# Graph attention and a top-2 expert network on one core: a new order of the attention steps, statistics of two tokens at once, a centred gate, and mixed tiles spread among the others

## The chip, the core and the metric

The kernel runs on one core of one Trainium2 chip. A core has five engines with instruction streams of their own: TensorE (PE, matmuls and transposes), VectorE (DVE), ScalarE (ACT), GpSimd (POOL) and SyncE (SP, which here issues DMAs). They meet only through semaphores. The metric is the device time of one execution in microseconds (us).

## The reference

There are 16384 tokens (128 graphs of 128 nodes) of 128 features, and 16 experts.

```python
def edge_score(a):
    s = jnp.einsum('bid,bjd->bij', hidden * a, hidden)
    return jax.nn.leaky_relu(s, LEAKY_SLOPE)
...
alpha = jnp.where(adj == 1, e0, NEG_INF)
alpha = jnp.where(adj == 2, e1, alpha)
...
alpha = jax.nn.softmax(alpha, axis=-1)
return jnp.matmul(alpha, hidden)
...
logits = jnp.einsum('bsd,de->bse', x, gate_w) + gate_b
probs = jax.nn.softmax(logits, axis=-1)
top_probs, top_idx = jax.lax.top_k(probs, 2)
...
h1 = jnp.einsum('bsd,edh->bseh', x, w1)
h2 = jnp.einsum('bsd,edh->bseh', x, w2)
hidden = jax.nn.silu(h1) * h2
expert_out = jnp.einsum('bseh,eho->bseo', hidden, w3)
...
x = x + _L0_gnn_ref(_layernorm(x, axis=-1), adj, L0_gnn_a0, ...)
x = x + _L0_ffn_ref(_layernorm(x, axis=-1), L0_ffn_gate_w, ...)
```

Each token needs only its two best experts.

## The kernel before

**Attention part.** The graphs are taken in 32 groups of four (`G`, `T`). `steps` writes the program of each engine step by step: in step `s` an engine does its work for several groups, each a fixed number of steps behind (`on(lag)`). The order inside a step is the order of the code, and each engine runs it strictly in turn. For a group, VectorE takes the statistics of each token (`bn_stats`, `bn_aggr`, L782 and L794), GpSimd makes scale and shift of them (`norm`, L533 to L546), ScalarE normalises (`h`, L624), TensorE transposes `h` into `psT` (L1004), and ScalarE copies that out as `hT` (L643) and four times scaled by `a0` to `a3` as `hTa` (L656). There is one buffer of each, so the scores of a group (L993, with the mask added by L997, into `psS`) must be done before those of the next are written. VectorE takes the largest of the four (L771, 2048 elements), the leaky slope (L788) and the row's maximum (L799), ScalarE the exponentials (L616). TensorE turns the probabilities (L1012) and multiplies (L1028), and VectorE adds the input (`x1`, L828). For the second layer norm there are statistics again (L844, L858), a normalised copy `x2` (L633), its transpose (L1020), the copy `x2T` (L653), the gate's matmul (L1058), `logit` (L850) and the two best experts (L865, L869). In every second step the places of two groups' tokens in their experts' lists are counted (L877 to L883, matmuls L1043 to L1049, L805 to L820). GpSimd then writes rows of 134 elements into `first_list` by indirect DMA (L559).

**Expert part.** Two passes (`r`), one for each of the two choices, have 72 tiles of 256 rows each. A *whole* tile belongs to one expert, a *mixed* one has two blocks of 128 rows with an expert each, a *lone* one holds the last incomplete blocks of two neighbouring experts. Each pass takes 48 whole, then 8 lone, then 16 mixed tiles, in turns of `S` = 8, with eight buffers (`xin`, `we`). SyncE reads a tile's word from a table with a register load (`value_load`, L398 and L401), loads its rows (L426 whole, L419 by blocks) and copies the expert's weights within SBUF into `we` (L415, 384 KB; a mixed tile does it twice). Buffer `u` is loaded again when its rows have been written out (`s_z[u]`). For tile `u` TensorE does the up-projections (L1101), then the transposes of tile `u + 1` (L1113), then the down-projection of tile `u - 1` (L1124). VectorE writes `hid` (L958), adds the result to the rows (L964) and, in the first pass, normalises the rows of tile `u + 2` (L971). GpSimd sends them to `second_list` (L571), in the second pass to the output (L583). The tiles of the first 4 turns are drawn from a list of the first 26 groups, so they can start before the others are sorted. Between the passes SyncE waits for the tiles with real rows, whose number for each buffer it reads from `real_i` (L466). ScalarE writes the padding rows during the tiles (L675, L680).

## Time and profile before

| what | us |
|---|---|
| median of 3 runs (822.02 to 825.97) | 824.17 |
| profiled execution | 820.67 |
| its span, first to last instruction | 818.7 |

| engine | busy us | share of the span |
|---|---|---|
| TensorE matmuls | 710.3 | 87% |
| TensorE weight loads | 572.1 | 70% |
| VectorE | 543.1 | 66% |
| ScalarE | 437.5 | 53% |
| GpSimd | 514.9 | 63% |

The shares are means over two parts with different limits, so each must be read by itself. A row of a timeline gives start, duration, engine, line, operation, what it writes and reads, and in brackets the idle time ahead of it with the engine or DMA that ended it. Merged rows (x4) span several instructions. The DMA engines moved 154.07 MB.

### The profile page before, as it was taken

How to read it: one execution, taken by the hardware profiler on the slowest of the kernel's cores; microseconds unless marked ns; L12 is line 12 of the kernel's file. 1: busy time of each engine (PE TensorE's matmuls, PEld its weight loads, DVE VectorE, ACT ScalarE, POOL GpSimd, SP SyncE). 2: the span in 40 equal slices, each digit the busy share in tenths (PEclk: the TensorE clock that was granted, in tenths of full speed). 3: DMA queues.
4: the chain of work that ended last, by engine and by line, in shares of the span. 5: the costliest groups of instructions: out<-in, count | busy, mean ns of one | idle time of the engine just before them, and what ended most of it. 6: DMA issues, size and time to landing. Idle time of an engine off the chain costs nothing.

```text
span 818.7 us, 17860 instructions
## 1 busy us (share of the span) xinstructions
PE 710.3 (87%) x4420; PEld 572.1 (70%) x4420; DVE 543.1 (66%) x2118; ACT 437.5 (53%) x1075; POOL 514.9 (63%) x664
## 2 busy tenths in 40 slices
PE   3788888888888887697999998977899999999872
PEld 1355555555555555586899998967799999999772
DVE  3779999999999999765666665543444444444231
ACT  4689999999999997232333332322233333333220
POOL 3124777777777777677767675654466666766443
PEclk9889999999999999589999999999999999999997
DMA  7233433332222210267999985888888888858880
GB/s 187 58 91 99 123 118 119 119 114 91 80 83 83 83 40 28 81 209 227 318 306 311 328 279 130 285 287 296 279 265 267 294 276 270 268 155 298 279 300 3
DMA packets 127449, 154.07 MB, mean 188 GB/s; under 512 B 16362, under 2 KB 98545, under 8 KB 127378
## 3 DMA queue, kind: packets, MB, share of 16 engines
q1 hardware_dynamic: 107008, 115.63, 44.5%
q0 software_dynamic: 15616, 34.38, 12.1%
q10 hardware_dynamic: 4754, 3.25, 1.3%
q8 instruction: 27, 0.44, 0.2%
q14 instruction: 44, 0.36, 0.2%
HBM read 52.28 MB, written 41.19 MB: 114 GB/s over the span
## 4 chain that ended last, share of the span: by engine, by line
POOL 28%; issue 27%; PE 20%; SPq 15%; DMA 4%; ACT 3%; DVE 1%; POOLq 1%; DVEq 0%; ACTq 0%
POOL first_list L559 14%; PE psS L1101 9%; SPq L419 5%; PE bank L1124 5%; POOL second_list L571 5%; SPq L415 5%; PE psS L993 4%; POOL norm L542 3%; SPq L401 3%; POOL out_dram L583 2%; ACT late L656 2%; DMA second_list<-xin 2%; PE bank L1113 1%; POOL stage L527 1%; POOL negmean L536 1%
## 5 line engine op out<-in xcount | busy, mean ns | idle before, releaser
L1101 PE MATMUL psS<-xT,late 128*128 128x256 f32 (+1 forms) x1280 | 249.8, 343 | 4.4 <-DMA late<-wts 2.3
L1101 PEld LDWEIGHTS psS<-xT,late 128*128 128x128 f32 x1280 | 202.7, 195 | 21.5 <-issue 4.5
L666 ACT ACTIVATE silu<-psS 128x512 f32<-128x512 f32 x144 | 86.0, 597 | 206.4 <-PE psS L1101 206.4
L583 POOL DMA_INDIRECT out_dram<-xin x144 | 141.6, 983 | 80.4 <-issue 53.5
L571 POOL DMA_INDIRECT second_list<-xin x144 | 141.9, 985 | 79.1 <-issue 52.0
L958 DVE TENSOR_TENSOR hid<-silu,psS 128x512 f32<-128x512 f32 x144 | 98.9, 687 | 134.5 <-PE psS L1101 127.9
L559 POOL DMA_INDIRECT first_list<-stage,slot x128 | 127.3, 994 | 50.3 <-issue 35.8
L993 PE MATMUL psS<-late,hT 128*128 128x512 f32 x256 | 126.6, 640 | 21.9 <-ACT late L656 20.8
L1124 PE MATMUL bank<-late,hid 128*128 128x128 f32 x1024 | 135.8, 276 | 0.1
L964 DVE SCALAR_TENSOR_TENSOR xin<-bank,xin 128x128 f32<-128x128 f32 x288 | 87.8, 346 | 70.3 <-PE bank L1124 64.9
L1124 PEld LDWEIGHTS bank<-late,hid 128*128 128x128 f32 x1024 | 124.6, 192 | 0.4 <-issue 0.4
L670 ACT ACTIVATE xT<-bank 128x256 f32<-128x256 f32 x144 | 55.4, 385 | 108.9 <-PE bank L1113 106.0
L993 PEld LDWEIGHTS psS<-late,hT 128*128 128x128 f32 x256 | 49.0, 202 | 76.8 <-issue 54.7
L771 DVE TENSOR_REDUCE late<-psS 128x512 f32<-128x2048 f32 x32 | 72.9, 2278 | 15.4 <-PE psS L997 14.0
L1113 PE MATMUL bank<-ident,xin 128*128 128x128 f32 x288 | 56.3, 277 | 28.5 <-DVE xin L971 18.2
L656 ACT ACTIVATE late<-bank,acol 128x512 f32<-128x512 f32 x128 | 76.9, 686 | 0.0
L1113 PEld LDWEIGHTS bank<-ident,xin 128*128 128x128 f32 x288 | 38.2, 143 | 42.5 <-issue 28.7
L971 DVE TENSOR_SCALAR xin<-xin 128x128 f32<-128x128 f32 x144 | 43.7, 375 | 24.9 <-DMA xin<-first_list 24.8
L624 ACT ACTIVATE h<-X,norm 128x128 f32<-128x128 f32 x128 | 52.7, 483 | 13.2 <-POOL norm L546 13.2
L542 POOL TENSOR_TENSOR norm<-veps,minus_half 128x8 f32<-128x8 f32 (+1 forms) x36 | 57.3, 1593 | 0.0
L533 POOL TENSOR_SCALAR veps<-mv 128x8 f32<-128x8 f32 (+1 forms) x36 | 9.5, 264 | 74.1 <-DVE mv L794 73.7
L633 ACT ACTIVATE x<-stage,norm 128x128 f32<-128x128 f32 x128 | 52.4, 480 | 4.1 <-POOL norm L546 4.1
(152 smaller groups left out, 913.4 us busy)
## 6 DMA issues: line engine op xcount, KB each, us to landing
late<-wts SPq DMA_DIRECT2D x160, 384.0 KB, 3.8
xin<-second_list SPq DMA_DIRECT2D x48, 262.0 KB
X<-in_x_dram SPq DMA_DIRECT2D x32, 256.0 KB, 2.9
late<-in_adj_dram SPq DMA_DIRECT2D x32, 256.0 KB, 3.4
xin<-first_list SPq DMA_DIRECT2D x48, 134.0 KB
xin<-second_list SPq DMA_DIRECT2D x48, 131.0 KB
wts<-in_L_ffn_w_dram SPq DMA_DIRECT2D x48, 128.0 KB
xin<-first_list SPq DMA_DIRECT2D x48, 67.0 KB
```

The source lines that it names most:

```text
L542: nc.gpsimd.tensor_tensor(norm[:, b, ln, :, 0], veps[:, b, ln, :], minus_half[:, ln, :], ALU.pow).then_inc(s_rs, 1)
L559: pool.indirect_dma_start(first_list[:, :], bass.IndirectOffsetOnAxis(ap=slot[:, g % SB, t:t + 1], axis=0), stage_v(g % SB)[:, t, :], None ...
L571: pool.indirect_dma_start(second_list[:, :], bass.IndirectOffsetOnAxis(ap=xin[:, u, k, SLOT1:SLOT1 + 1].bitcast(i32), axis=0), xin[:, u, k ...
L583: pool.indirect_dma_start(out_rows[:, :], bass.IndirectOffsetOnAxis(ap=xin[:, u, k, DEST:DEST + 1].bitcast(i32), axis=0), xin[:, u, k, 0:D ...
L656: last = nc.scalar.activation(hTa[:, k, :], psT[:, :], ACT.Copy, scale=acol[:, k:k + 1])
L666: nc.scalar.activation(silu[:, w, :], psG[w], ACT.Silu).then_inc(s_silu[u % TURNS], 1)
L958: v.tensor_tensor(hid[:, w, :], silu[:, w, :], psU[w], ALU.mult).then_inc(s_hid[u % TURNS], 1)
L964: last = v.scalar_tensor_tensor(at, psY[1 - w][:, t * D:(t + 1) * D], xin[:, k, t, GATE[r]:GATE[r] + 1], at, ALU.mult, ALU.add)
L993: mm(psS[:, t, :], hT[:, t * D:(t + 1) * D], hTa[:, :, t * D:(t + 1) * D], start=True, stop=False)
L1101: last = mm(out[:, c * W2 + rows.start:c * W2 + rows.stop], at[:, half * H + c * P:half * H + (c + 1) * P], xT[:, w, rows], start=True, st ...
L1113: last = nc.tensor.transpose(psX[1 - w][:, t * P:(t + 1) * P], xin[:, k, t, ROW:ROW2], ident[:, :])
L1124: last = mm(psY[1 - w][:, t * D:(t + 1) * D], hid[:, 1 - w, at:at + P], at_down[t][:, c * D:(c + 1) * D], start=(c == 0), stop=(c == HC - 1))
```

## The change

Attention part. `h` is normalised a step earlier: `steps` begins at -1, and statistics and `h` are those of group `s + 1`. TensorE transposes group `s` ahead of the scores of group `s - 1`. `hT` and `hTa` have two buffers, and ScalarE writes them ahead of the exponentials. Statistics are taken of two tokens with one instruction: their elements are read in turn, so that the even and the odd halves that `bn_stats` keeps are the two tokens' own, and `bn_aggr` goes. The gate is centred: the weights less their column means (`gwc`, made once) are applied to the transposed `x1` itself, and the scale is applied to the result (`scaled`), so `x2` goes. 

On ScalarE, one step of the attention part of before, `late<-late,negmax` being the exponentials, `late<-bank,acol` the scaled copies `hTa`, `x` the second normalised rows:

```order
L604 ACTIVATE late<-late 128x512
L616 ACTIVATE late,rowsum<-late,negmax 128x128 x4
L624 ACTIVATE h<-X,norm 128x128 x4
L633 ACTIVATE x<-stage,norm 128x128 x4
L643 ACTIVATE hT<-bank 128x512
L648 ACTIVATE probT<-bank 128x512
L653 ACTIVATE x2T<-bank 128x512
L656 ACTIVATE late<-bank,acol 128x512 x4
```

and the same step in the changed kernel:

```order
L613 ACTIVATE late<-late 128x512
L624 ACTIVATE hT<-bank 128x512
L626 ACTIVATE late<-bank,acol 128x512 x4
L634 ACTIVATE late,rowsum<-late,negmax 128x128 x4
L643 ACTIVATE h<-X,norm 128x128 x4
L651 ACTIVATE probT<-bank 128x512
L656 ACTIVATE x1T<-bank 128x512
```

The turned and scaled copies moved from the end of the step to its head, and the second normalisation is gone. On VectorE, from the reduction of the scores to the best experts in a step of before that does no counting:

```order
L771 TENSOR_REDUCE late<-psS 128x512
L777 RECIPROCAL rinv<-rowsum 128x4
L782 BN_STATS stats<-X 128x6 x4
L788 SCALAR_TENSOR_TENSOR late<-late 128x512
L794 BN_AGGR mv<-stats 128x2 x4
L799 TENSOR_REDUCE negmax<-late 128x4
L828 SCALAR_TENSOR_TENSOR stage<-bank,rinv,X 128x128 x4
L836 TENSOR_SCALAR late<-late 128x512 x4
L844 BN_STATS stats<-stage 128x6 x4
L850 TENSOR_TENSOR logit<-bank,gbias 128x64
L858 BN_AGGR mv<-stats 128x2 x4
L865 MAX best<-logit 128x8 x4
```

and in the changed kernel:

```order
L775 TENSOR_REDUCE late<-psS 128x512
L781 RECIPROCAL rinv<-rowsum 128x4
L747 BN_STATS stats<-X 128x6 x2
L793 SCALAR_TENSOR_TENSOR late<-late 128x512
L800 TENSOR_TENSOR scaled<-bank,norm 128x64
L806 TENSOR_REDUCE negmax<-late 128x4
L812 TENSOR_TENSOR logit<-scaled,gbias 128x64
L841 SCALAR_TENSOR_TENSOR stage<-bank,rinv,X 128x128 x4
L849 TENSOR_SCALAR late<-late 128x512 x4
L747 BN_STATS stats<-stage 128x6 x2
L865 MAX best<-logit 128x8 x4
```

Both aggregations went, four statistics became two, and the gate's sums take two operations, moved ahead of `x1`.

Expert part. `S` is 12, so there are twelve buffers. Only the up-projection's weights are copied (`UP` = 512 columns, 256 KB); the down-projection reads `wts` in place, at an address that TensorE takes from the table itself. In each pass the first 36 tiles are whole, the next 31 are 12 whole, 8 lone and 11 mixed ones spread evenly, and the last 5 are mixed. The tiles of the first 3 turns (36 tiles) come from the early list. Only these turns are loops; the others are written out. Places in the table count rows instead of blocks. SyncE reads five of the counts between the passes instead of eight. ScalarE writes the paddings during tiles 4 to 35. VectorE normalises tile `u + 2` ahead of adding the result of tile `u - 1`. On TensorE, the last whole and the first two lone tiles of before (`psS` is the up-projection, `bank<-ident,xin` the transposes, `bank<-late,hid` and `bank<-wts,hid` the down-projection):

```order
L1113 MATMUL bank<-ident,xin 128x128 x2
L1124 MATMUL bank<-late,hid 128x128 x4
L1136 REGISTER_ALU
L1136 COMPARE_AND_BRANCH
L1101 MATMUL psS<-xT,wts 128x128 x8
```

and in the changed kernel a lone tile behind a mixed one, of the 31 spread ones:

```order
L1117 MATMUL psS<-xT,wts 128x128 x8
L1088 TENSOR_LOAD table_i x2
L1131 MATMUL bank<-ident,xin 128x128 x2
L1141 REGISTER_ALU x2
L1141 ISA
L1141 MATMUL bank<-wts,hid 128x128
L1141 ISA
L1141 MATMUL bank<-wts,hid 128x128
```

Between the up-projection and the transposes stands a register load for each block of the tile before it (one for a whole tile), and register arithmetic ahead of the down-projection. The core of the diff:

```diff
-    S = 8
...
+    S = 12
+    SURE = (TOKENS - E * (W2 - 1)) // W2
+    PAIRS = TOKENS // W2 - SURE
...
+    LAST = 5
...
+    first = EARLY_TURNS * S
+    TILE = wholes[:first] + spread(mixed[:-LAST], spread(lones, wholes[first:])) + mixed[-LAST:]
...
-            for s in range(G + LAST_LAG):
+            for s in range(-1, G + LAST_LAG):
...
-                sp.dma_start(we[:, u, a, :], wts[:, ds(e * EW, EW)]).then_inc(s_we[u], 16)
+                sp.dma_start(we[:, u, a, :], wts[:, ds(e * EW, UP)]).then_inc(s_we[u], 16)
...
-                    wait(pool, s_ag1, min(s + 1, G))
-                    wait(pool, s_ag2, s - 3)
-                    nc.gpsimd.tensor_scalar(veps[:, b, ln, :], mv[:, b, ln, :, 1], EPS, None, ALU.add
+                    wait(pool, s_st1, min(s + 2, G))
+                    wait(pool, s_st2, s - 3)
+                    nc.gpsimd.tensor_scalar(veps[:, b, ln, :], stats[:, b, ln, :, 2], 1.0 / D, EPS, ALU.mult, ALU.add
...
+                if on(0):
+                    act.wait_ge(s_hTp, s + 1)
+                    wait(act, s_S, s - 1)
+                    nc.scalar.activation(hT[:, s % 2, :], psT[:, :], ACT.Copy)
+                    for k in range(K):
+                        last = nc.scalar.activation(hTa[s % 2][:, k, :], psT[:, :], ACT.Copy, scale=acol[:, k:k + 1])
+                    last.then_inc(s_hT, 1)
...
+            def two_stats(b, ln, t, rows):
+
+                return v.bn_stats(stats[:, b, ln, t:t + 2, :].rearrange("p t c -> p (t c)"), rows)
...
+                    for t in range(0, T, 2):
+                        last = two_stats(s % 2, 0, t, X[:, g % XQ, t * D:(t + 2) * D].rearrange("p (t d) -> p d t", t=2))
...
+                    v.tensor_tensor(scaled[:, :, :], psL[:, ds(h0 * T * E, T * E)].rearrange("p (t e) -> p t e", t=T),
+                                    norm[:, (s + 1) % 2, 1, :, 0:1].to_broadcast([P, T, E]), ALU.mult
+                                    ).then_inc(s_scaled, 1)
...
-                        last = mm(psL[:, c:c + E], x2T[:, t * D:(t + 1) * D], gwt[:, :],
+                        last = mm(psL[:, c:c + E], x1T[:, t * D:(t + 1) * D], gwc[:, :],
...
+            def experts_whole(r, j):
+                return [expert(pe.value_load(table_i[0:1, ds(2 * j, 1), r]))] * 2
...
+                if experts:
+                    e = experts()
                 if ahead:
...
-                                      at_down[t][:, c * D:(c + 1) * D],
+                                      wts[:, ds(e[t] * EW + (UP + c * D), D)],
```

## Rows read from the trace of the kernel before

**Rows 1.** Table of stretches: start:end, length, then busy us of each engine, clock, DMA.
```profile
100.00:200.00 100.00, 87.27 (x467) 55.39 (x468) 99.24 (x472) 94.57 (x251) 73.17 (x110) 1.00 0.37 113
```
**Rows 2.** Timeline of VectorE, one attention step: start us, us, operation, out<-in.
```profile
137.50 2.27 DVE L771 TENSOR_REDUCE late<-psS 128x512 f32<-128x2048 f32 x1
139.78 0.84 DVE L782 BATCH_NORM_STATS2 stats<-X 128x6 f32<-128x128 f32 x4
...
141.13 0.37 DVE L794 BATCH_NORM_AGGREGATE mv<-stats 128x2 f32<-128x6 f32 x4
...
147.18 2.28 DVE L771 TENSOR_REDUCE late<-psS 128x512 f32<-128x2048 f32 x1
```
**Rows 3.** Timeline of TensorE, starts of the up-projections of single tiles (L1101).
```profile
349.06 3.78 PE L1101 MATMUL psS<-xT,late 128*128 128x256 f32 x8 [0.47 <-ACT xT L670]
...
487.69 1.89 PE L1101 MATMUL psS<-xT,late 128*128 128x256 f32 x8
490.53 1.89 PE L1101 MATMUL psS<-xT,late 128*128 128x256 f32 x8
496.37 1.95 PE L1101 MATMUL psS<-xT,wts 128*128 128x128 f32 x16
...
528.25 1.95 PE L1101 MATMUL psS<-xT,late 128*128 128x128 f32 x16
...
583.40 1.97 PE L1101 MATMUL psS<-xT,late 128*128 128x256 f32 x8 [0.58 <-issue]
...
751.64 1.95 PE L1101 MATMUL psS<-xT,late 128*128 128x128 f32 x16
...
800.63 1.95 PE L1101 MATMUL psS<-xT,late 128*128 128x128 f32 x16
```
**Rows 4.** Timeline of SyncE among the mixed tiles: row loads of successive blocks.
```profile
538.74 0.35 SPq L419 DMA_DIRECT2D xin<-first_list  x1
...
540.63 0.34 SPq L419 DMA_DIRECT2D xin<-first_list  x1
```
**Rows 5.** ScalarE's register loads (L674): ns min/median/max; all sixteen, then one.
```profile
L674 ACTq TENSOR_LOAD <-padrow x16: 287/672/1087, 404.8 to 447.3; - x16
...
L674 ACTq TENSOR_LOAD <-padrow x1: 287/287/287, 441.7 to 441.7; - x1
```
**Rows 6.** Timeline of ScalarE, the activation ahead of that one load.
```profile
441.61 0.39 ACT L670 ACTIVATE xT<-bank 128x256 f32<-128x256 f32 x1 [0.48 <-PE bank L1113]
```
**Rows 7.** Groups by line and form, 100 to 293.5 us: count | busy us, mean ns.
```profile
L616 ACT ACTIVATE late<-late,negmax 128x128 f32<-128x128 f32 x80 | 31.1, 390 | 1.9 <-DVE negmax L799 0.9
...
L883 DVE TENSOR_REDUCE takensum<-onehot 128x32 f32<-128x256 bf16 x10 | 5.8, 584 | 0.3
...
L820 DVE TENSOR_REDUCE slot<-hit 128x8 int32<-128x128 f32 x10 | 2.7, 275 | 0.0
```
**Rows 8.** Timeline of TensorE, transposes, product, counting and gate of one step.
```profile
145.98 0.66 PE L1004 MATMUL bank<-ident,h 128*128 128x128 f32 x4
...
148.47 1.16 PE L1028 MATMUL bank<-h,probT 128*128 128x128 f32 x8 [0.30 <-ACT probT L648]
149.47 0.27 PE L1043 MATMUL bank<-base,unit 128*128 128x256 bf16 x1
...
150.20 0.96 PE L1058 MATMUL bank<-gwt,x2T 128*128 128x16 f32 x8
```
**Rows 9.** Timeline of ScalarE, normalisation, turned copy, scaled copies of one step.
```profile
144.28 1.65 ACT L624 ACTIVATE h<-X,norm 128x128 f32<-128x128 f32 x4 [0.52 <-POOL norm L546]
...
147.37 0.57 ACT L643 ACTIVATE hT<-bank 128x512 f32<-128x512 f32 x1
...
148.81 2.39 ACT L656 ACTIVATE late<-bank,acol 128x512 f32<-128x512 f32 x4
```
**Rows 10.** Timeline of TensorE, scores of the second and the sixth group.
```profile
22.69 5.40 PE L993 MATMUL psS<-late,hT 128*128 128x512 f32 x8 [3.00 <-ACT late L656]
...
64.39 3.70 PE L993 MATMUL psS<-late,hT 128*128 128x512 f32 x8 [0.84 <-ACT late L656]
```

More of the change, by code:

```diff
@@ L209, in gnn_then_moe @@
         s_st1 = sem("s_st1")
-        s_ag1 = sem("s_ag1")
         s_ve = sem("s_ve")
@@ L335, in tiles @@
                     between(j)
[L336 to L342 removed]
+            with eng.Fori(at, last) as n:
+                for u in range(S):
+                    body(n, u, lambda d: True)
             for j in range(last * S, end + 1):
@@ L1092, in tile, with expert, experts_early, experts_of @@
-            def tile(r, n, u, weights, down, ahead=True, own=True):
+            def expert(word):
+                return (word >> BITS) & (E - 1)
+            def experts_early(r, j):
+                return [expert(pe.value_load(etable_i[0:1, ds(2 * j, 1)]))] * 2
+            def experts_whole(r, j):
+                return [expert(pe.value_load(table_i[0:1, ds(2 * j, 1), r]))] * 2
+            def experts_of(r, j):
+                kind, i = TILE[j]
+                if kind == "lone":
+                    return [2 * i, 2 * i + 1]
+                if kind == "mixed":
+                    return [expert(pe.value_load(table_i[0:1, ds(2 * SURE + 2 * i + a, 1), r])) for a in range(2)]
+                return (experts_whole if r or j >= EARLY_TURNS * S else experts_early)(r, i)
@@ L1093, in tile @@
+            def tile(r, n, u, weights, experts, ahead=True):
                 w = u % 2
-                if own:
+                if weights:
                     done(pe, s_hid, n, u, -2)
                     done(pe, s_xT, n, u, 0)
-                    parts = weights(r, n, u)
+                    parts = weights()
                     for half, out, s_out in ((0, psG[w], s_G), (1, psU[w], s_U)):
```

412 lines of the change are left out of this document (196 added, 216 removed).

## The prediction

> **What bounds the kernel now.** The program has two parts. The attention part (32 groups of four graphs) runs to about 345 us; then 144 tiles of the expert network run to the end. I read the table of stretches first. Between 100 and 200 us VectorE is busy 99.24 us of 100, ScalarE 94.57 and TensorE 87.27 [rows 1]. So VectorE sets the pace there, and the other two are close behind. The timeline of one group's work on VectorE shows no idle time between 137.50 and 147.18 us: one step takes 9.68 us, and a row's last 0.08 us or so lie under the next operation [rows 2].
>
> For the tiles I read the starts of the up-projection matmuls. Whole tiles start 2.84 us apart (487.69, 490.53), lone and mixed tiles 2.90 apart where nothing stops them (496.37 to 528.25 is 11 of them) [rows 3]. At that pace 143 intervals would take 408.9 us: 96 whole tiles by 2.84 and 47 others by 2.90. They take 800.63 - 349.06 = 451.6 [rows 3]. The missing 42.7 us are four pieces: 8.0 among the first 48 tiles (141.5 for 47 intervals of 2.84), 3.0 at the first lone tile (5.84 instead of 2.84), 17.5 in the last 13 intervals of the first pass (55.15 against 37.7), and 14.2 in the last 12 of the second (48.99 against 34.8). TensorE bounds the tiles otherwise.
>
> **The tiles, part by part.** *Mixed tiles.* SyncE issues two loads of rows and two copies of weights for each, one pair every 1.89 us [rows 4]: 3.8 us a tile, against TensorE's 2.90. Sixteen stand in a row at the end of each pass, so TensorE catches up with SyncE however much lead there was. That explains the third and fourth pieces. The new order puts eleven of them among 12 whole and 8 lone tiles. A whole tile costs SyncE about one pair (2.0 with its longer row load), and a lone one two row loads without a copy, some 2.5. The 31 tiles then cost 11 x 3.8 + 12 x 2.0 + 8 x 2.5 = 86 us of SyncE against 31 x 2.88 = 89 of TensorE: level. The five mixed tiles left at the end lose 5 x 0.9 = 4.5 us of lead. With twelve buffers instead of eight a load can go out about 20 us ahead of its tile (twelve tiles are 34 us; some 11 of them pass from a tile's up-projection until its rows are written out, and a few go to the landing). So SyncE no longer stops TensorE inside a pass. The weights that are copied shrink from 384 KB to 256, which also takes load off the DMA engines.
>
> *First tiles.* Eight buffers run out while GpSimd is still sending the last attention rows. Twelve last until its queue has caught up. Of the 8.0 us I keep 2, the start at the low clock, and remove 6. The 3.0 at the first lone tile goes too: there SyncE read eight registers in a row before it loaded. Now it reads five, with a lead of many tiles.
>
> *Between the passes.* The second pass still must not load before the last real row of the first is written. The stalled mixed tiles that used to cover this are gone. Routing the reference's inputs fills 120 units of 128 rows in the first pass; 96 go into whole tiles, so the twelfth of the 16 mixed tiles, the first of the five at the end, is the last with rows. From its up-projection to its written rows is about 11 us, and a load, a transpose and a copy follow: I count 3 us of idle TensorE. Kept in all: 2 + 3, and 3 more for single stalls. So the tiles take 417, a gain of 42.7 - 8 = 34.7 us.
>
> *TensorE's new register reads.* Each down-projection now reads its weights at an address that TensorE's own sequencer fetches: one register load for a whole tile, two for a mixed one, none for a lone one, and some register arithmetic. No row shows such a load on TensorE. The nearest are ScalarE's: 287 to 1087 ns, middle 672 [rows 5]. They stand behind the up-projection, whose eight matmuls occupy the array for about 1.7 us, and ahead of the transposes. One load of 0.7 and 0.3 of arithmetic fit under that; two just fit. What matters is that a register load does not wait for its engine to finish. One on ScalarE took 287 ns from 441.7, while the activation from 441.61 ran 0.39 us [rows 5, 6]: it ended first. So I cost it at 0 for whole tiles and about 0.1 for mixed ones, within the 3 above. The ends are 0 and one full load and the arithmetic, 1.0 a tile, uncovered.
>
> **The attention part.** VectorE loses, twice a step, four statistics of 128 elements (0.84 busy, 0.76 with the overlap taken off) and four aggregations (0.37, or 0.29) [rows 2]: 2.10 us. It gains one product of 64 elements (0.12 of its own, half the elements of one 0.19 statistic) and four statistics of 256 elements, which read two tokens in turn, 512 bytes apart. No row shows that form. Two bounds: 256 contiguous elements would be one step of 128 (0.76 / 4 = 0.19) plus 128 more at about 1.04 ns each (2048 elements in 2.27 us, 0.14 of it fixed) [rows 2], so 0.33. The reduction of 256 elements that strides through SBUF takes 584 ns where one of 128 contiguous elements takes 275 [rows 7]. At 1.04 ns an element the longer should take 275 + 133 = 408, so its elements cost 1.7 ns. With that the new instruction is 0.50. Doubling the time of each element, the upper end, gives 0.59.
>
> The Trainium skill speaks against the change here: SBUF — State Buffer, Door 1: The DMA port swizzle, says that accesses to one 16-byte line run at full bandwidth and each crossing to a new line pays. The strided reduction agrees. By the rule the new statistics cost 0.50 or more, by full-speed reads 0.33; whether two lines that are read in turn pay, no row tells.
>
> I take 0.50, since the row is an SBUF read of the same length, though of 16-bit data. VectorE's step is then 9.68 - 2.10 + 0.12 + 4 x 0.50 = 9.70: unchanged. With 0.33 it would be 9.0, with 0.59 10.06.
>
> Not all of a gain would show. In the new order ScalarE scales the turned rows of a group directly behind its transposes, then takes the exponentials, then normalises the next group, then copies the turned probabilities; TensorE multiplies these, does the counting matmuls in every second step and the gate, and only then transposes the next group. This is a loop: 0.66 transposes [rows 8], 0.48 + 2.30 turned and scaled copies [rows 9], 4 x 0.39 exponentials [rows 7], 1.56 normalisation, 0.57 copy [rows 9], 1.00 product, 0.96 gate [rows 8] and some 0.1 of signals, 9.2 us, and 0.73 more in every second step [rows 8]: 9.55. The tails that I counted whole may bring it to 9.4. It replaces the old wait for the scaled copies, and it is the floor at 0.33. The removed second normalisation (1.6 us of ScalarE) therefore buys little: it is filled with waiting for TensorE.
>
> So the steady steps give 0 to 1 us. The early steps run slower: four of them take 41.7 us from the scores at 22.69 to those at 64.39, 10.4 each, on matmuls at the low clock [rows 10], and there the scores and the scaled copies that share one buffer wait for each other. Double buffering saves some 0.5 a step, 2 in all, and at the end the gate no longer waits for a normalisation: 1 more, less the extra group ahead at the start. I take 3 us for the part.
>
> **Sum.** 34.7 + 3 = 37.7. The profiled execution took 820.67 us (818.7 span and 2.0 around it), which becomes 783.0. The median of the three runs is 824.17, 3.5 above it, which gives 786.5.
>
> **Rivals.** *Statistics at full speed* (0.33): the loop of 9.4 to 9.5 bounds instead, 0.2 to 0.3 less in some 26 steps, so 7 us less: 779.5. For it: the reduction of scores strides through PSUM at full speed [rows 2]; against: the SBUF row [rows 7].
>
> *Statistics slower than 0.50*: at 0.59 the step grows by 0.36, in 26 steps 9 us: 796. For it: the 32-bit data and the 512-byte stride could cost more than 16-bit data did.
>
> *SyncE stays behind in the mixed tiles.* If the lead is used up, since register loads of 0.5 to 0.9 us crowd in, up to half of the 31.7 us of both ends stays: 800. Against it: the account above, 86 against 89 with 20 us in hand.
>
> *TensorE waits for its registers*, the way to slower. If a register load on TensorE waited until the array is empty, or if addresses from registers made each down matmul issue slowly, every whole and mixed tile (128 of them) would grow. It decides from 37.7 / 128 = 0.29 us a tile. At the full 1.0 us it gives 128 more: 914. For it: the pair of matmul and weight load leaves only 0.11 us each in the down-projection, and the transposes follow at once. Against: the 287 ns on ScalarE, and TensorE's sequencer runs ahead of the array.
>
> **How the numbers follow.** My forecast 0.54; full-speed statistics 0.22; slow statistics 0.08; SyncE behind 0.09; TensorE's registers 0.07, of which 0.06 lies beyond the point and so slower. The range is 772 to 808: it holds the first four and their bounds. Faster by over 0.5% (about what a measurement of this kernel can tell from no change): 0.93; within it 0.01; slower 0.06.
>
> **What would show it.** In the profile after: up-projections 2.84 and 2.90 apart through the mixed tiles and a gap of 3 us between the passes; the wait of the transposes for VectorE's normalised rows nearly gone; the new statistics at about 0.58 us each by their row (0.41 for the fast rival, 0.67 for the slow one); VectorE without idle time in the attention part, steps of 9.6 to 9.7. Under the fast rival VectorE shows idle time ahead of its statistics or its reduction and TensorE waits for the copied probabilities. Whole tiles more than 2.9 apart would make the forecast of the tiles wrong; a middle with gaps ahead of transposes would put it on SyncE.

## The result, and the profile of the changed kernel

The changed kernel took 770.25 us (median of 769.1, 770.13, 770.36 and a slow 1043.2, whose granted clock was 0.65 instead of 0.97 and which the ratio leaves out) against 823.1 for the kernel before on the same chip: a ratio of 0.935, 95% interval [0.931, 0.940]. That is 52.9 us less, where I forecast 37.7. Its profiled execution took 770.36 us with a span of 768.1. By spans the gain is 818.7 - 768.1 = 50.6 us, and it divides so:

| part | before | after | gain | forecast |
|---|---|---|---|---|
| start to the first tile | 349.06 | 334.20 | 14.9 | 3 |
| first to last tile (143 intervals) | 451.57 | 414.55 | 37.0 | 34.7 |
| last tile's start to the end | 18.07 | 19.35 | -1.3 | 0 |

The first ten experiments ran on three chips on which the kernel before took 935 to 947 us and the tiles of every variant stood 3.9 to 4.2 us apart in the mean (2.90 here), so of those only comparisons within one chip and the attention part are used, whose mean step for the same instructions is 9.33 to 9.39 us on all the chips; the last eight ran on two chips where the kernel before took 822.

*Attention part.* The same table of stretches as [rows 1] (start:end, length, busy us of TensorE matmuls and weight loads, VectorE, ScalarE, GpSimd; clock, DMA, GB/s):

```profile
100.00:200.00 100.00, 87.50 (x494) 56.41 (x493) 96.06 (x371) 79.39 (x222) 80.40 (x114) 1.00 0.39 116
```

VectorE fell from 99.24 to 96.06 and ScalarE from 94.57 to 79.39, in steps that are themselves shorter. The new statistics by their line, 100 to 280 us (ns min/median/max; two instructions a step for each of the two):

```profile
L747 DVE BATCH_NORM_STATS2 stats<-X x38: 393/406/422, 104.2 to 272.6; 128x6 f32<-128x256 f32 x38
L747 DVE BATCH_NORM_STATS2 stats<-stage x38: 408/419/429, 109.8 to 278.1; 128x6 f32<-128x256 f32 x38
```

That is the 0.41 us that the full-speed rival named, not the 0.58 of my forecast. VectorE's timeline of two steps (start, us, engine, line, operation; in brackets the idle time ahead and what ended it), where [rows 2] had none:

```profile
139.29 2.27 DVE L775 TENSOR_REDUCE late<-psS 128x512 f32<-128x2048 f32 x1
...
141.57 0.72 DVE L747 BATCH_NORM_STATS2 stats<-X 128x6 f32<-128x256 f32 x2
142.22 0.67 DVE L793 SCALAR_TENSOR_TENSOR late<-late 128x512 f32<-128x512 f32 x1
143.43 0.22 DVE L800 TENSOR_TENSOR scaled<-bank,norm 128x64 f32<-128x64 f32 x1 [0.54 <-PE bank L1064]
...
148.78 2.27 DVE L775 TENSOR_REDUCE late<-psS 128x512 f32<-128x2048 f32 x1
...
157.95 2.28 DVE L775 TENSOR_REDUCE late<-psS 128x512 f32<-128x2048 f32 x1
```

The steps take 9.49 and 9.17 us in turn, 9.33 in the mean, against 9.68. In the longer one VectorE waits 0.54 us for the gate's matmuls (L1064). Who waits for whom, 100 to 280 us (engine and line, what it waited for: us in total, times, longest):

```profile
ACT hT L624 <- PE bank L997: 35.4, 19, 2.2
...
PEld bank L1033 <- ACT probT L651: 22.0, 19, 1.2
...
DVE scaled L800 <- PE bank L1064: 5.4, 10, 0.5
```

ScalarE waits 1.9 us in each step for the next group's transposes, and TensorE more than a microsecond for the copied probabilities: the two wait for each other in turn, which is the loop that the prediction describes.

*Tiles.* Starts of up-projections on TensorE (first tile; last of the first pass; first of the second; last), as [rows 3]:

```profile
334.20 3.78 PE L1117 MATMUL psS<-xT,late 128*128 128x256 f32 x8 [0.47 <-ACT xT L669]
...
539.99 1.95 PE L1117 MATMUL psS<-xT,late 128*128 128x128 f32 x16
...
545.13 1.97 PE L1117 MATMUL psS<-xT,late 128*128 128x256 f32 x8 [0.58 <-ACT xT L669]
...
748.75 1.95 PE L1117 MATMUL psS<-xT,late 128*128 128x128 f32 x16
```

Of 143 intervals only five are longer than 2.95 us: 4.68 and 3.41 at the start, 5.14 between the passes, and 2.98 and 3.00. Whole tiles stand 2.84 apart, lone and mixed ones 2.90, everywhere. TensorE bounds the tiles from end to end.

### The profile page after: what moved, and what is told of

Its sections match the earlier page's. It is cut to its first block, busy times and chain, and to the rows that moved or that the text cites. A ratio compares the mean times of both kernels' runs of the same rounds, so it can differ in the third digit from the quotient of the medians.

```text
span 768.1 us, 17656 instructions
## 1 busy us (share of the span) xinstructions
PE 690.5 (90%) x4422; PEld 564.0 (73%) x4423; DVE 517.6 (67%) x1770; ACT 384.9 (50%) x946; POOL 530.7 (69%) x668
## 3 DMA queue, kind: packets, MB, share of 16 engines
q1 hardware_dynamic: 107008, 94.66, 41.5%
q0 software_dynamic: 15616, 34.38, 13.1%
## 4 chain that ended last, share of the span: by engine, by line
PE 55%; ACT 20%; issue 13%; POOL 8%; DVE 2%; DMA 0%; POOLq 0%; ACTq 0%; DVEq 0%
PE psS L1117 25%; PE bank L1141 12%; POOL out_dram L592 8%; ACT late L626 8%; ACT late L634 5%; PE bank L1033 5%; ACT h L643 4%; PE bank L1064 4%; PE bank L1131 3%; ACT probT L651 2%; PE bank L997 2%; PE psS L1005 2%; PE bank L1052 1%; DMA X<-in_x_dram 0%; PE psS L1009 0%
## 5 line engine op out<-in xcount | busy, mean ns | idle before, releaser
L1117 PE MATMUL psS<-xT,late 128*128 128x256 f32 (+1 forms) x1280 | 247.3, 341 | 2.1 <-ACT xT L669 1.5
L1117 PEld LDWEIGHTS psS<-xT,late 128*128 128x128 f32 x1280 | 199.8, 192 | 19.0 <-issue 1.8
L568 POOL DMA_INDIRECT first_list<-stage,slot x128 | 133.2, 1040 | 50.1 <-issue 37.2
L1141 PE MATMUL bank<-wts,hid 128*128 (+1 forms) x1152 | 152.4, 275 | 0.7 <-issue 0.7
L1141 PEld LDWEIGHTS bank<-wts,hid 128*128 128x128 f32 x1152 | 140.0, 192 | 1.0 <-issue 1.0
L1005 PE MATMUL psS<-late,hT 128*128 128x512 f32 x256 | 118.5, 607 | 2.0 <-DVE late L775 2.0
L1033 PE MATMUL bank<-h,probT 128*128 128x128 f32 x256 | 38.0, 293 | 27.4 <-ACT probT L651 27.4
L551 POOL TENSOR_TENSOR norm<-veps,minus_half 128x8 f32<-128x8 f32 (+1 forms) x37 | 61.5, 1663 | 0.0
L1033 PEld LDWEIGHTS bank<-h,probT 128*128 128x128 f32 x256 | 31.8, 195 | 35.0 <-ACT probT L651 35.0
L634 ACT ACTIVATE late<-late,negmax 128x128 f32<-128x128 f32 x128 | 50.0, 415 | 6.4 <-DVE negmax L806 6.4
```

The source lines that it names most:

```text
L568: pool.indirect_dma_start(first_list[:, :], bass.IndirectOffsetOnAxis(ap=slot[:, g % SB, t:t + 1], axis=0), stage_v(g % SB)[:, t, :], None ...
L634: last = nc.scalar.activation(prob[:, p, c], prob[:, p, c], ACT.Exp, bias=negmax[:, p, t:t + 1], accum_out=rowsum[:, p, t:t + 1])
L1005: mm(psS[:, t, :], hT[:, g % 2, t * D:(t + 1) * D], hTa[g % 2][:, :, t * D:(t + 1) * D], start=True, stop=False)
L1033: last = mm(psO[:, c], probT[:, c], h[:, g % HB, c], start=True, stop=True)
L1117: last = mm(out[:, c * W2 + rows.start:c * W2 + rows.stop], at[:, half * H + c * P:half * H + (c + 1) * P], xT[:, w, rows], start=True, st ...
L1141: last = mm(psY[1 - w][:, t * D:(t + 1) * D], hid[:, 1 - w, at:at + P], wts[:, ds(e[t] * EW + (UP + c * D), D)], start=(c == 0), stop=(c = ...
```

## Experiments on the attention part

The scores' reduction on VectorE (the 2.27 us row) opens each step, so its starts time the steps. In the table, *first five* is the sum of the first five intervals, *step* the mean from the 9th to the 29th start, and *all* the time from the first to the 32nd.

| kernel | first five | step | all |
|---|---|---|---|
| before | 50.4 | 9.68 | 301.1 |
| before_two_tokens | 48.6 | 9.46 | 293.6 |
| before_two_buffers | 48.4 | 9.87 | 304.1 |
| one_token | 41.5 | 9.68 | 290.8 |
| changed kernel | 42.6 | 9.33 | 283.9 |
| after_control (the same again) | 40.9 | 9.34 | 282.3 |
| in_a_row | 40.9 | 9.39 | 283.2 |
| turn_ahead | 39.2 | 9.19 | 277.4 |
| turn_scaled | 40.7 | 8.98 | 272.5 |

The undisturbed intervals of one_token are 9.50 and 9.74 in turn, 9.62 in the mean; one of its intervals is 10.7. Those of before_two_tokens are 9.17 and 9.68, 9.42 in the mean. The two traces of the same changed kernel differ by 1.7 us in the first five, all of it in the first interval (8.71 and 7.01), so a difference of that size there says nothing.

**in_a_row: does reading two tokens in turn cost anything?**

```
- two_stats(s % 2, 0, t, X[:, g % XQ, t * D:(t + 2) * D].rearrange("p (t d) -> p d t", t=2))
+ two_stats(s % 2, 0, t, X[:, g % XQ, t * D:(t + 2) * D])
```

and the same for `stage`. This mixes the tokens' statistics, so tokens go to other experts, and only its attention part can be compared.

> The changed kernel, but each statistic reads its two tokens one behind the other (256 elements in a row, so that even and odd elements of both are mixed, and the normalisation uses wrong numbers; the work is otherwise the same). Theory A (reading two lines in turn costs nothing, and VectorE is no longer the bound): the rows of the statistics stay at 0.41 to 0.42 us, steps 9.33, time 770 within 1. Theory B (the turns cost something): the rows fall, to 0.33 or so, but the time stays within 2 of 770, since the loop of ScalarE and TensorE sets the steps.

The rows read:

```profile
L747 DVE BATCH_NORM_STATS2 stats<-X x38: 389/402/423, 103.2 to 272.4; 128x6 f32<-128x256 f32 x38
L747 DVE BATCH_NORM_STATS2 stats<-stage x38: 404/415/424, 108.6 to 277.8; 128x6 f32<-128x256 f32 x38
```

4 ns less, 1%. Its steps of 9.39 are those of tiles_in_rows and loads_6 (9.39 and 9.38), which have the changed kernel's attention part on another of the first three chips. Two lines read in turn, 512 bytes apart in `X` and 536 in `stage`, cost VectorE nothing that matters. Theory A holds.

**one_token: the statistics of before in the changed kernel.** Four `bn_stats` of one token and four `bn_aggr` in place of two two-token ones, in both normalisations, with the waits of before.

> The changed kernel with the statistics of the kernel before: one bn_stats for each token and four bn_aggr, in both normalisations. VectorE gets 2.10 - 4 x 0.33 = 0.78 us more a step. Theory A (the loop of ScalarE and TensorE sets the 9.33 us, VectorE has 0.3 to 0.4 us left): steps of 9.7 to 9.8, 0.4 x 26 = 10 to 12 us more, 781. Theory B (VectorE still sets the step): steps of 10.1, 20 us more, 790.

925.67 us, and 916.05 for in_a_row on the same chip: 9.6 more, of which 7.6 lie in the attention part (290.8 against 283.2). Steps of 9.62 where nothing disturbs them, against 9.39; from 100 to 280 us VectorE was busy 178.57 us of 180. So it is VectorE that sets the step there, with some 0.2 us more than the loop. Theory A, a little under its numbers.

**before_two_tokens: the statistics alone in the kernel before.** The mirror of it: `two_stats` in place of L782, L794, L844 and L858, nothing else.

> The kernel before with the two-token statistics alone (order, gate and tiles as they were). VectorE's step falls from 9.68 by 0.78 to 8.9. Theory A (the statistics alone were worth the steady part; ScalarE with its 9.15 us of work is the next bound): steps of 9.2 to 9.4, 8 to 13 us less than before, 811 to 815. Theory B (the new order was needed, since the wait for the one buffer of scaled copies takes the place of VectorE): steps of 9.6, no more than 3 us gained.

Steps of 9.46 (9.2 and 9.7 in turn), and 7.5 us less from the first to the last of the attention part; whole executions took 931.83 against 934.68, ratio 0.992 [0.988, 0.997], 2.9 us less, on a chip where the tiles take longer and vary. VectorE and ScalarE were both busy 171.6 us of 180: two engines at 95% that wait for each other. Between the theories, nearer to A: 0.2 us a step came, not 0.3 to 0.5.

The four corners (301.1, 293.6, 290.8, 283.9) add up as far as they can be read: the statistics are worth 7.5 us alone and 6.9 on top of the rest, the new order with its double buffers and centred gate 10.3 and 9.7. Each holds single long steps and the uncertain first interval, so 2 us either way are open. Of the 10.3, 8.9 lie in the first five steps, of the 9.7, 5.9. The undisturbed later steps (9.68, 9.42, 9.62, 9.33 to 9.39) are clearer: there the statistics bring 0.2 to 0.3 us a step and all the rest less than 0.1. The centred gate by itself was not tried.

**before_two_buffers: the buffers alone.**

```
- wait(act, s_S, g)
- nc.scalar.activation(hT[:, :], psT[:, :], ACT.Copy)
+ wait(act, s_S, g - 1)
+ nc.scalar.activation(hT[:, s % 2, :], psT[:, :], ACT.Copy)
```

with `hT` and `hTa` twice.

> The kernel before with two buffers for the turned and the scaled copies (hT, hTa), nothing else. Theory A (what made the early steps short in the changed kernel is the order: TensorE turns the next group ahead of the scores, so that the scores leave the loop): no step changes, since the next copies still wait for transposes that stand behind the scores; 0 to 1 us. Theory B (the step as I predicted it: the scores and the scaled copies wait for each other over the one buffer): the first five steps lose 0.5 us each or more, 2 to 5 us in all.

936.48 against 936.91, ratio 0.998 [0.994, 1.002]. Its first five intervals are 8.0, 10.2, 10.1, 9.0 and 11.1 (before: 9.7, 10.2, 10.1, 10.7, 9.7). The later ones are 9.6 to 9.8 with single ones of 10 to 11.2. The three traces of the new order on this chip have none of these, and the kernel before was not traced there, so they stay unexplained. The 1.7 us of the first interval is not the buffers' either: the second group's scores took 3.70 us there and 5.40 in the kernel before, so TensorE's clock was at its upper level. In 17 traces of the changed kernel and its variants the same scores took 5.37 in six and 3.67 in eleven, and these two lengths differ even between the changed kernel and after_control, the same program. So the buffers alone bring nothing that can be seen; theory A.

What shortens the first steps must be in the rest of the change, most likely that TensorE turns group `s` ahead of the scores of group `s - 1`. The scores then leave the loop, and this goes with two things. First 22.69 to 64.39, four groups in 41.7 us [rows 10], against 24.48 to 59.34 in the changed kernel, 34.9; second, TensorE's clock. Its scores there, with those of the third group:

```profile
24.48 5.37 PE L1005 MATMUL psS<-late,hT 128*128 128x512 f32 x8 [2.04 <-DVE late L775]
33.26 3.60 PE L1005 MATMUL psS<-late,hT 128*128 128x512 f32 x8
```

From the third group on they take 3.60 us instead of 5.37: the clock is at its upper level. The table of stretches gives a granted clock of 1.00 from 30 us on; in the kernel before it is 0.83 from 20 to 60 us and the scores take 5.40 up to the one that starts at 53.73. How much of the 7 us is the clock, before_two_tokens tells in part, since it has the old order and its clock was up for two groups (scores, as above):

```profile
33.26 3.70 PE L980 MATMUL psS<-late,hT 128*128 128x512 f32 x8 [1.15 <-ACT late L654]
41.75 3.70 PE L980 MATMUL psS<-late,hT 128*128 128x512 f32 x8 [1.15 <-ACT late L654]
51.42 5.40 PE L980 MATMUL psS<-late,hT 128*128 128x512 f32 x8 [0.81 <-ACT late L654]
```

These are 8.49 and 9.67 us apart, where the kernel before has 10.19 and 10.67 at the lower level (its interval ahead of them, at the lower level in both, is 10.18 in both) and the changed kernel 8.13 and 8.97 at the upper. If the fourth interval gains as the third does, the clock accounts for 1.7 + 1.0 + 1.0 = 3.7 us and the order, with whatever the gate and the missing normalisation do in it, for the other 3.1, by my estimate. In all 17 traces of the new order the scores of the third to the ninth group are at the upper level; in the three of the old order scores at the lower level occur up to the fifth or sixth. Why the clock holds in one order and not in the other, no run shows.

**turn_ahead: is the loop of ScalarE and TensorE really the bound?** TensorE's transposes of the next group moved ahead of the product with `h`:

```
+ if on(-1):  pe.wait_ge(s_h, s + 2); wait(pe, s_hT, s + 1)
+     for t in range(T): transpose(psT[...], h[:, (s + 1) % HB, ...], ident)   -> s_hTp
  if on(2):   pe.wait_ge(s_probT, g + 1) ... psO = probT x h
```

(and removed from the head of the step).

> The changed kernel, but TensorE transposes the next group ahead of the product with h, the counting and the gate, so these three leave the loop of ScalarE and TensorE (2.0 us of it, 2.7 in every second step). Theory A (that loop is the bound): VectorE's own 9.0 us become the bound, 0.25 to 0.3 less in some 28 steps: 762 to 764, and TensorE's turned rows are there before ScalarE asks. Theory B (VectorE's work and its hand-overs are the bound): no change, 769 to 771.

910.91 against 916.05 for in_a_row on the same chip: 5.1 less. Steps of 9.19, against 9.39 on that chip and 9.33 in the changed kernel. ScalarE's wait for the transposes is gone. The direction of theory A, a little under its 0.25 to 0.3 a step, so the loop was the bound but another stood 0.14 to 0.2 us behind it. The waits name it: every second step VectorE still stops for the gate, and ScalarE now for the row's maximum (100 to 280 us):

```profile
ACT late L634 <- DVE negmax L806: 20.7, 20, 1.4
...
DVE scaled L800 <- PE bank L1064: 3.3, 9, 0.5
```

**turn_scaled: that wait taken out as well.** On VectorE the second pair of statistics goes behind the leaky slope, the maximum ahead of `scaled`, the bias behind `x1`:

```
  red, rinv, - stats(0), stats(2), leaky, scaled, negmax, logit, ... x1
  red, rinv, + stats(0), leaky, stats(2), negmax, scaled,        ... x1, logit
```

> The version with the next group's transposes ahead of the product (as in turn_ahead), and on VectorE the product of the gate's sums with the scale (scaled) moved behind the row's maximum, so that it no longer waits for the gate's matmuls; the bias is added later, and the second pair of statistics stands between the leaky slope and the maximum. Theory A (that wait of 0.37 in every second step, and the maximum that ScalarE waits for, are what was left): steps of 9.0 to 9.05 against 9.34, 9 to 10 us less than the changed kernel, ratio to it 0.988 to 0.99. Theory B (another loop of 9.2 is behind it): steps stay at 9.2, 5 us less.

757.19 us (756.06 to 761.91) against 769.92 (769.3 to 770.1) for the changed kernel on the same chip, 12.7 less, a ratio of 0.983; against the kernel before 0.921 [0.917, 0.925]. The stretch of 100 to 280 us:

```profile
100.00:280.00 180.00, 164.02 (x908) 108.19 (x904) 178.96 (x701) 152.72 (x412) 140.11 (x211) 1.00 0.33 99
```

VectorE is busy 178.96 of 180 and the list of waits has none of its own. Steps of 8.98, where I had worked out 9.0 for VectorE at full-speed statistics. Theory A. By spans it is 11.7 us (755.4 against 767.1): 9.9 from the first reduction to the last, 0.4 ahead of the first, 1.0 between the last and the first tile, 0.4 in the tiles; the expected 9 to 10 were those of the steps alone. This version beats both kernels.

## Experiments on the tiles

The changed kernel has three choices that the kernel before has not: twelve buffers, the spread sequence, and copies of 256 KB. (It also writes most tiles out instead of looping.) The undone choices, each a line or two:

```
- TILE = wholes[:first] + spread(mixed[:-LAST], spread(lones, wholes[first:])) + mixed[-LAST:]
+ TILE = wholes + lones + mixed                                       # rows
- S = 12
+ S = 8                                                               # eight
- sp.dma_start(we[:, u, a, :], wts[:, ds(e * EW, UP)])
+ sp.dma_start(we[:, u, a, :], wts[:, ds(e * EW, EW)])                # wide
```

> The changed kernel with the tiles in the old sequence, 48 whole, 8 lone, 16 mixed in each pass. Theory A (SyncE's 3.8 us for a mixed tile against TensorE's 2.9 is a loss of 14.4 us in 16 of them, of which the four more buffers, 11.4 us, take the most): 3 us lost at each end, 776. Theory B (the spreading is what counts, the lead is used up by the landing of the loads): 10 us and more at each end, 790 or more. Theory C (the smaller copies and the buffers do it alone): 770.

> The changed kernel with S = 8 instead of 12: eight buffers, turns of eight, the first 32 tiles from the early list, the others spread as before with five mixed ones at the end. Theory A (the buffers bought the first tiles and the ends): 6 us more among the first 48 tiles and 2 to 3 at each end, 781. Theory B (spreading and smaller copies did all): 770 to 772.

916.18 and 920.54 us, with 915.49 for a kernel of the same chip that came out equal to the changed one (loads_6, below): on that chip nothing was to be learned of the first, and little of the second. Both again on a chip where the kernel before takes 822 us, then the other combinations:

> The tiles in the old sequence (48 whole, 8 lone, 16 mixed) with twelve buffers, once more. Where transfers are undisturbed: theory A (buffers take most of the 14.4 us that SyncE falls behind in 16 mixed tiles), 3 us lost at each end, 776; theory B (the spreading counts), 10 us and more at each end, 790 or more. Where tiles of all variants stand 3.9 us apart: within 0.5% of after_control.

> Eight buffers instead of twelve, once more. Where transfers are undisturbed: 6 us more among the first 48 tiles, 2 to 3 at each end, 781. Where tiles of all variants stand 3.9 us apart: 0.3 to 1% above after_control, since fewer buffers cover less of each stall.

> The changed kernel, for comparison on the same chip: 770 on an undisturbed chip, 915 to 925 on one like those of the last ten runs.

> The changed kernel with the old sequence of tiles and eight buffers, the copies still 256 KB. SyncE's pair of row load and copy took 1.72 us in tiles_in_rows_2 (473.82, 475.55, 477.27), so a mixed tile 3.45 against 2.9, 8.8 us behind in 16. Theory A (with eight buffers the lead is some 9 to 10 us less than with twelve): the old sequence now costs 5 to 9 us at each end, 790 to 797. Theory B (the sequence never mattered): 779, as eight_buffers_2.

> Eight buffers, the new sequence, copies of 384 KB. Theory A (bytes cost through SyncE's pair, 1.89 instead of 1.72, which the spread sequence hides): 779 to 783. Theory B (the DMA engines, busy 0.8 already with 256 KB in the tiles, are what the bytes cost, in every sequence): 790 or more.

> The same, and each copy takes the expert's whole 384 KB, as in the kernel before (the down-projection still reads in place). All three old choices together. Theory A (sequence, buffers and bytes account for the tiles): the tiles take about 450 us again, 805 to 808. Theory B (something else, the written-out tiles or the earlier register loads, carries part): 10 us or more less than that.

| buffers | sequence | copies | kernel | us | 143 intervals |
|---|---|---|---|---|---|
| 12 | spread | 256 KB | after_control | 769.92 | 414.0 |
| 12 | rows | 256 KB | tiles_in_rows_2 | 769.88 | 416.8 |
| 8 | spread | 256 KB | eight_buffers_2 | 779.27 | 425.2 |
| 8 | spread | 384 KB | eight_wide | 784.39 | 427.1 |
| 8 | rows | 256 KB | rows_eight | 792.39 | 438.2 |
| 8 | rows | 384 KB | rows_eight_wide | 797.92 | 444.7 |
| 8 | rows | 384 KB | before, its profile | | 451.6 |

The first three rows come from one chip, the next three from another (the kernel before took 822.1 and 821.6 there). The buffers bought most. With twelve the sequence is worth 0.0 us; with eight it is worth 13.1. The bytes are worth 5.1 or 5.5 by the medians, 1.9 or 6.5 by the intervals of the profiled executions. Neither theory of tiles_in_rows_2 held: 3 us at each end was too much. SyncE's timeline there says why (row loads of successive blocks in the mixed tiles, as [rows 4]):

```profile
475.55 0.35 SPq L430 DMA_DIRECT2D xin<-first_list  x1
...
477.27 0.34 SPq L430 DMA_DIRECT2D xin<-first_list  x1
...
478.96 0.35 SPq L430 DMA_DIRECT2D xin<-first_list  x1
...
480.83 0.35 SPq L430 DMA_DIRECT2D xin<-first_list  x1
```

A pair takes 1.76 us in the mean of these, so a mixed tile 3.5 against 2.9, and 16 of them put SyncE 10 us behind. Four more buffers give a lead of 4 x 2.85 = 11.4. Only the gap between the passes is longer (first tile of the second pass 6.68 and second 4.45 behind, together 3 us more than in the changed kernel, with a wait for a copy of weights). That is in the profiled execution, the slowest of four (772.67 us), and not in the median. With eight buffers the same deficit comes out. TensorE's up-projections at the end of rows_eight's first pass:

```profile
524.19 1.95 PE L1117 MATMUL psS<-xT,late 128*128 128x128 f32 x16
532.00 2.99 PE L1117 MATMUL psS<-xT,late 128*128 128x128 f32 x16
535.94 1.95 PE L1117 MATMUL psS<-xT,late 128*128 128x128 f32 x16
```

7.81 us instead of 2.90, and then 3.94. The waits of 500 to 580 us name what came late, the rows, which VectorE normalises ahead of the transposes:

```profile
DVE xin L967 <- DMA xin<-first_list: 17.8, 9, 5.3
```

The step of the prediction on the first tiles held: eight_buffers_2 needs 142.1 us for its first 47 intervals and after_control 135.8, so the buffers removed 6.3 there (5.5 against the changed kernel's first trace, 136.6; I said 6.0). eight_wide, at 784.39, lies 1.4 above the numbers of its theory A and 5.6 below those of B, so a busy share of 0.8 of the DMA engines is not what limits the tiles in the main. rows_eight_wide fell 7 to 10 us below its theory A: all three choices together leave 444.7 us of intervals where the kernel before had 451.6. 3.0 of the difference is the stall at the first lone tile, which it does not have, and 4.9 the last 12 intervals (44.1 against 48.99 [rows 3]). What gives the latter, the written-out tiles, the down-projection in place or another of the remaining differences, is open.

**TensorE's register loads.**

> The changed kernel with six more register loads on TensorE's sequencer for each tile, ahead of the transposes (their values are not used). A load there takes 0.30 to 0.36 us by its row. Theory A (the sequencer runs ahead of the array, and about 1.7 us of queued up-projection cover it): seven loads take 2.5 us, 0.8 of it uncovered, 0.8 x 142 = 110 us more. Theory B (the loads overlap each other or more is queued than I think): under 20 us more. Theory C (each load would cost its own time): 6 x 0.36 x 142 = 300 us more.

915.49 us, but the six loads were not in the program: the trace has TensorE's 160 register loads and the 17656 instructions of the changed kernel, so loads whose value nothing uses had been dropped. It serves as a control. The next kernel uses them:

```
+ def again(load):
+     word = load()
+     for _ in range(3): word = word | load()
+     return word
- return [expert(pe.value_load(table_i[0:1, ds(2 * j, 1), r]))] * 2
+ return [expert(again(lambda: pe.value_load(table_i[0:1, ds(2 * j, 1), r])))] * 2
```

> The changed kernel with every register load of TensorE's sequencer made four times (four for a whole tile, eight for a mixed one, their words combined by or). One load takes 0.30 to 0.36 us by its row, the arithmetic about 0.05. Theory A (the sequencer runs ahead of the array by the queued up-projection, about 1.7 us): whole tiles 1.5 us of loads, covered, no change; mixed tiles 2.9, 1.2 of it uncovered in 32 tiles: 38 us more. Theory B (each load costs its own time): 3 x 0.35 in 96 whole and 6 x 0.35 in 32 mixed tiles: 168 us more. Theory C (more is queued than the up-projection): no change in either.

> The changed kernel as it is, on the chip of the other kernels of this call. If this chip lets the transfers through as the first one did, the ratio is 0.935. If it is like the two chips of the last eight runs, where the kernel before took 935 us and tiles of all variants stood about 3.9 us apart, the attention part (15 us) and little of the tiles remains: about 915, a ratio of 0.98.

961.61 and 924.31 us: 37 more, which was theory A's 38 by accident. The intervals don't fit it, since whole tiles had grown too, and among 3.9 us intervals much is hidden. Hence once more:

> Every register load of TensorE's sequencer four times, once more on a chip where transfers may be undisturbed. The run before gave 37 us more than its control, with whole tiles at 3.27 instead of 2.91 us (first quartile). Theory A (about 1.1 us are covered, four loads and their arithmetic are 1.5): whole tiles 3.2 to 3.3 apart, mixed ones (eight loads, 2.9 us) more, 96 x 0.4 + 32 x 1.8 = 96 us more or less of what stalls would not hide: 850 to 870. Theory B (1.7 us are covered): whole tiles unchanged, 38 us more, 808.

912.02 us against 769.92, 142 more (another chip of the same kind; before 821.57). An interval in which TensorE fetches for a whole tile (four loads) is 3.37 us in the median, one in which it fetches for a mixed tile (eight) 5.34, and 4.7 to 5.5, 5.05 in the mean, where mixed tiles stand in a row at the ends. TensorE in the mixed tiles (end of the second pass):

```profile
873.14 0.41 PE L1138 MATMUL bank<-ident,xin 128*128 128x128 f32 x2 [0.87 <-issue]
873.88 1.50 PE L1148 MATMUL bank<-wts,hid 128*128 x8 [0.33 <-issue]
875.22 1.95 PE L1124 MATMUL psS<-xT,late 128*128 128x128 f32 x16
```

It stops for nothing but its own sequencer, ahead of the transposes and again ahead of the down-projection. Eight loads at 0.30 us (row below) and, by my estimate, some 0.6 of arithmetic are 3.0 us, of which 2.15 show in the rows at the ends and 2.4 elsewhere; four are 1.5, of which 0.5 show. So 0.6 to 1.0 us are covered, most often some 0.9, not the 1.7 of the up-projection that I counted.

```profile
L1094 PEldq TENSOR_LOAD <-table_i x40: 297/304/702, 591.5 to 615.3; - x40
```

The cost in the changed kernel is still nothing: one load and its arithmetic are 0.4 us, the mixed tiles' two 0.75, and their tiles stand 2.90 apart like the lone ones, which have none. But the margin is some 0.15 us, by this estimate. Had a load taken the 0.67 that I read on ScalarE [rows 5], the two of a mixed tile would have shown.

## Why the prediction was wrong, point by point

The direction and the large term were right; the time lies 1.8 us below the range, and 16.3 below the forecast. 3.6 of these come from the last step of the sum: I added 3.5 for the distance between the profiled execution before and the median of three, and the changed kernel's profiled execution lies at its median. The other 12.7 are these.

- **Missing 42.7 us in four pieces, 8 kept.** 5.6 remain: 2.4 at the start (2 said), 2.2 between the passes (3 said), the rest single stalls (3 said). The term is off by 2.3.
- **Mixed tiles.** The step "TensorE catches up with SyncE however much lead there was" is wrong. The lead of twelve buffers is more than the 10 us by which SyncE falls behind, so the spreading that my account rested on was worth nothing here; it is worth 13 us only with eight. My 86 against 89 was true but not needed.
- **First tiles.** Right: 6.3 for 6.0.
- **TensorE's register reads, 0 and 0.1.** Right in the result, and the reason right in kind: the sequencer runs ahead. The cover was mis-sized, some 0.9 us for 1.7, and the duration too, 0.30 for 0.67. I took the latter from ScalarE's sixteen loads; SyncE's 128 loads from the tile table, in the same trace (L401), took 253/270/866 ns and were the nearer row.
- **Statistics at 0.50.** This is the step that failed. I carried a strided reduction's 1.7 ns an element over to `bn_stats`. Its rows show 0.41 with start-up, 0.33 net, so VectorE had 9.0 us and not 9.70, and the later steps gained 9.4 us in all, where I had put 0 to 1. The rival at full speed, to which I gave 0.22, is what happened: TensorE waits for the copied probabilities, steps take 9.33 where it said 9.4 to 9.5, and VectorE has idle time, though ahead of the gate's sums and not ahead of the statistics or the reduction, as it said. Its time of 779.5 is 9 us too high all the same, for the early steps, the tiles and the 3.5 that I added at the end. The Trainium skill (SBUF — State Buffer, Door 1: The DMA port swizzle) would have each crossing to a new 16-byte line pay; in_a_row shows 4 ns for 256 elements of which each lies in another line than the last. By that rule the forecast would have stood; the measurement decides against it for this pattern.
- **Early steps, 2 us.** The second failed term. The reductions of the first five steps came 7.8 us closer together, which with the 9.4 us of the later steps and 0.4 at the end makes 17.6, less 2.7 for the extra group ahead of the first. I named the double buffer as the reason. before_two_buffers shows nothing from it that the same program doesn't show from run to run. By my estimate above, about half is the new order, through the scores that leave the loop, and about half the clock, which rose 30 us earlier in these two traces; for the latter I had no term. One interval of 1.7 us is a matter of the execution: the first five take 40.9 us in after_control and 42.6 here.
- **End.** 1.3 us longer, for which I had no term. GpSimd issues its last transfer to the output 8.2 us behind the last tile's start in both (800.63 and 808.86; 748.75 and 756.98); what follows takes 11.1 us instead of 9.8. In the four kernels with eight buffers the end takes 18.4 us, and 19.4 with twelve, so 1.0 of it comes with the buffers; how, was not followed.

In sum, attention 11.9 above my 3, tiles 2.3 above, end 1.3 below: 12.9 by spans, 12.6 by execution times.

## What to carry to other kernels

Before an instruction's price is taken from a row of another operation, look for what that row has that the new one has not (here the data type and the operation), and give the price that the operation's own rows suggest the larger chance. When a step lengthens or shortens, write down every loop of engines through it, with each member's order, and ask which is next: here 9.68, 9.33, 9.19 and 8.98 lay behind one another, and the last two were bought by moving instructions without adding or removing any. Buffers, order and bytes that fight the same deficit don't add: compare the deficit (10 us) with the lead (11.4) first. And look at a second trace of the same kernel before a difference of 2 us early in the program is given a cause.

## What the runs showed of the hardware

- `bn_stats` over 256 32-bit elements takes 0.406 us contiguous or not (0.402 in a row), while the reduction that strides through 16-bit data still takes 0.59 to 0.60. So leaving a line with each read does not by itself slow VectorE; whether the operation, the data type or the shorter stride (64 bytes) slows the reduction was not tried.
- A register load from SBUF takes TensorE's sequencer 0.30 us. By the estimate above some 0.9 us of them a tile hide behind the array, and four times as many loads cost 142 us.
- Two engines can be 95% busy each and still leave 0.45 us a step to each other (before_two_tokens), and one 99.4% busy (turn_scaled) sets the step: 8.98 us, where its rows add up to 9.0.
- Which of its two levels TensorE's clock has early in a program can differ between two executions of the same kernel (second group's scores 5.37 us in one trace and 3.67 in the other), and it moves a step by 1.7 us. In the old order scores at the lower level occur up to the fifth or sixth group in all three traces; in the new one they took 3.60 to 3.68 us from the third to the ninth group in all 17.
- After some stalls among the tiles the next matmuls are slow as well: 2.99 instead of 1.95 us in the tile behind the 7.81 of rows_eight, where the granted clock was 0.64, and 3.78 instead of 1.89 in the first tile. After the 5.14 between the passes they were not (1.97).
